# A two-layer decoder kernel: router jobs in three units, shorter fillers, and a third set of split expert weights made two passes ahead

## The reference

```python
x = ln(x + self_attention(x))                 # 4 heads
x = ln(x + cross_attention(x, ctx))           # 16 heads
x = ln(x + moe_0(x))                          # 8 experts, top 2, F = 1024
x = ln(x + state_space(x))                    # h = exp(d*A)*h + (d*x)*B ; y = h.C
x = ln(x + linear_attention(x, ctx))          # softmax over keys, k^T v, q (k^T v)
# last sub-layer: 8 experts, top 2, F = 512, and one expert that all tokens pass
probs = softmax(xt @ Wg); topv, topi = top_k(probs, 2); topv /= topv.sum()
y  = gelu(xt @ Wu[e]) @ Wd[e]                 # for the two chosen e
x  = ln(x + gelu(xt @ W1) @ W2 + sum(topv * y))
```

## Time and profile before

| | us |
|---|---|
| median of 3 runs (lowest, highest) | 1577.16 (1569.95, 1578.38) |
| the profiled execution | 1579.87, its span 1578.1 |
| state-space units, from the first scan to the last | 1025 to 1287 |
| tail of the state-space stage | 1287 to 1318 |
| `m1`, first transpose on PE to the end | 1318 to 1578 |
| `m1`, routed double tiles (transposes of tile 10 to those of tile 24) | 1391 to 1516 |

### The profile page before, as it was taken

One profiled execution on the slowest core, in us unless ns is written; L12 is line 12 of the kernel. 1 busy time (PEld: TensorE's weight loads), 2 busy tenths in 40 slices (PEclk: granted clock), 3 DMA queues, 4 the chain that ended last, 5 costly groups with the idle time before them and its releaser, 6 DMA issues.

```text
span 1578.1 us, 27783 instructions
## 1 busy us (share of the span) xinstructions
PE 1387.3 (88%) x9328; PEld 1122.2 (71%) x9328; DVE 1100.6 (70%) x2430; ACT 933.1 (59%) x2302; POOL 828.2 (52%) x866
## 2 busy tenths in 40 slices
PE   4788999999999999966999999778989989998891
PEld 3566677777777777654999999445556558988881
DVE  4677866666666766647688884599989964766535
ACT  4666565655655655532688871277778843466553
POOL 3665454444444444531688872278868761265540
PEclk9889999999999999956999999989999999999896
DMA  4100000000000000045566568645443411245574
GB/s 147 41 28 7 21 15 8 2 7 2 8 8 1 8 1 2 1 142 221 184 235 218 206 220 295 243 147 162 142 128 129 140 46 54 94 161 180 182 246 174
DMA packets 52943, 167.87 MB, mean 106 GB/s; under 512 B 13178, under 2 KB 22340, under 8 KB 44996
## 3 DMA queue, kind: packets, MB, share of 16 engines
q1 hardware_dynamic: 45316, 145.63, 26.4%
q0 software_dynamic: 7488, 20.46, 4.0%
HBM read 149.28 MB, written 16.78 MB: 105 GB/s over the span
## 4 chain that ended last, share of the span: by engine, by line
PE 34%; DVE 7%; POOL 6%; issue 5%; ACT 4%; DMA 1%; POOLq 0%; DVEq 0%; SPq 0%; ACTq 0%
PE m_ps L1751 10%; PE m_ps L1774 10%; POOL s_hc L2073 4%; PE m_ps L1748 2%; PE m_ps L1769 2%; PE s_yps L2504 1%; PE m_ps L1731 1%; DVE s_h L2439 1%; PE s_dps L2615 1%; ACT s_dps L2152 1%; PE s_yps L2610 1%; DVE tokens L1619 1%; PE s_jps L2538 1%; PE m_ps L1699 1%; PE m_ps L1655 0%
## 5 line engine op out<-in xcount | busy, mean ns | idle before, releaser
L306 POOL TENSOR_TENSOR a_pexp<-a_pexp,a_rsum 128x384 f32<-128x384 f32 (+1 forms) x320 | 246.4, 788 | 303.3 <-DVE a_rsum L523 303.3
L396 ACT ACTIVATE a_pexp<-a_ps,a_nmax 128x384 f32<-128x384 f32 (+1 forms) x320 | 181.1, 566 | 171.8 <-DVE a_nmax L519 171.2
L519 DVE TENSOR_REDUCE a_nmax<-a_ps 128x1 f32<-128x384 f32 (+1 forms) x320 | 153.9, 522 | 71.8 <-PE a_ps L620 70.8
L2073 POOL TENSOR_TENSOR s_hc<-s_h,s_bc_rows 128x1024 f32<-128x1024 f32 x64 | 151.2, 2366 | 55.6 <-DVE s_h L2439 53.0
L1751 PE MATMUL m_ps<-m_xT,m_w1s 128*128 128x256 f32 x960 | 151.2, 297 | 16.6 <-issue 13.3
L2439 DVE TENSOR_TENSOR_SCAN s_h<-s_dps,s_inp 128x512 f32<-128x512 f32 x128 | 148.8, 1204 | 0.0
L1751 PEld LDWEIGHTS m_ps<-m_xT,m_w1s 128*128 128x128 f32 x960 | 133.9, 203 | 19.3 <-issue 15.1
L636 PE MATMUL a_ps<-a_ident,a_pexp 128*128 128x128 f32 x896 | 144.7, 274 | 3.4 <-ACT a_pT L255 3.0
L1099 POOL DMA_INDIRECT m_xrow<-table,m_row_from x78 | 81.1, 1040 | 125.7 <-DVE m_row_from L1446 90.1
L1774 PE MATMUL m_ps<-m_w2s,m_hs 128*128 128x256 f32 x960 | 143.1, 285 | 0.0
L2504 PE MATMUL s_yps<-s_hc,s_ident 128*128 128x512 f32 x256 | 124.5, 609 | 12.4 <-POOL s_hc L2073 12.0
(11 more groups left out here) (450 smaller groups left out, 3660.0 us busy)
## 6 DMA issues: line engine op xcount, KB each, us to landing
s_bc_rows<-s_bc_table SPq DMA_DIRECT2D x64, 512.0 KB, 3.7
arrived<-in_down SPq DMA_DIRECT2D x29, 1024.0 KB, 6.4
arrived<-in_up SPq DMA_DIRECT2D x23, 1024.0 KB
m_w<-in_up SPq DMA_DIRECT2D x16, 512.0 KB
m_w<-in_down SPq DMA_DIRECT2D x16, 512.0 KB
carried_up<-in_up SPq DMA_DIRECT2D x8, 512.0 KB, 5.5
carried_down<-in_down SPq DMA_DIRECT2D x8, 512.0 KB, 6.2
arrived<-results SPq DMA_DIRECT2D x3, 1024.0 KB, 8.5
```

Source lines behind the costliest of these rows:

```text
L306: nc.gpsimd.tensor_tensor(pexp[:, r, 0:n], pexp[:, r, 0:n], rsum[:, r:r + 1].to_broadcast([128, n]), ALU.mult).then_inc(normed, 1)
L396: nc.scalar.activation(pexp[:, r, 0:n], ps_s[score_bank(u)][:, 0:n], ACT.Exp, bias=nmax[:, r:r + 1], accum_out=sums[:, r:r + 1]).then_inc( ...
L519: nc.vector.tensor_reduce(nmax[:, u % RING:u % RING + 1], ps_s[score_bank(u)][:, 0:keys_of(u)], AX.X, ALU.max, negate=True).then_inc(maxed, 1)
L2073: nc.gpsimd.tensor_tensor(halves(hc[:, u % HC_RING, :]), halves(h[:, u % H_RING, :]), bc_rows[:, u % BC_RING, 1, :].unsqueeze(1).to_broadc ...
```

## The change

Three edits. The router's jobs G0, G1 and H stand in three units, G0 of chunk c - 1 in unit 15, G1 of chunk c - 2 in unit 0, H of chunk c - 2 in unit 4; for chunk 2, G0 is in unit 63 and G1 and H both in the tail. The fillers of the tail are 2 and 9 dummy matmuls, not 10 and 20. In the second expert layer there are three sets of split weights, and chunk ft of tile j + 2 is cast and subtracted in pass j, not that of tile j + 1. The first expert layer keeps two sets and one pass.

```diff
+    W_SETS = 3 if shared else 2
+    LOOK = W_SETS - 1
...
-        w1s = [... for b in range(2)]
+        w1s = [... for b in range(W_SETS)]
...
-            return (n, n // 2, n % 2) if routed(j) else (0, 0, 0)
+            return (n, n // 2, n % W_SETS) if routed(j) else (0, 0, 0)
...
             if shared:
-                for c in range(FT):
-                    low_part(TILES_SHARED, c)
+                for n in range(LOOK):
+                    for c in range(FT):
+                        low_part(TILES_SHARED + n, c)
...
-                    if j + 1 < TILES:
-                        low_part(j + 1, c)
+                    if j + LOOK < TILES:
+                        low_part(j + LOOK, c)
...
-                        act_e.wait_ge(h_used, tile * FT + 1)
+                        act_e.wait_ge(h_used, (tile + 2 - W_SETS) * FT + 1)
...
-                    if new_weights(j + 1):
-                        high_part(weights_of(j + 1), j + 1, ft)
+                    if new_weights(j + LOOK):
+                        high_part(weights_of(j + LOOK), j + LOOK, ft)
...
-                    if new_weights(j + 1) and on_dve(weights_of(j + 1)[0], ft) and split_weights(weights_of(j + 1)[0]):
+                    if new_weights(j + LOOK) and on_dve(weights_of(j + LOOK)[0], ft) and split_weights(weights_of(j + LOOK)[0]):
...
-        LOGITS_AT, COLUMNS_AT = 0, 15
+        ROUTER_JOBS = {15: ("G0", 1), 0: ("G1", 2), 4: ("H", 2)}
...
+        def router_jobs_at(u):
+            return [(job, u // N - behind) for job, behind in [ROUTER_JOBS[u % N]] if u // N >= behind] if u % N in ROUTER_JOBS else []
...
-                if c >= 2 and n == LOGITS_AT:
-                    logits(c - 2)
...
-                if c >= 1 and n == COLUMNS_AT:
-                    for half in range(2):
-                        router_columns(c - 1, half)
+                for job, of in router_jobs_at(u):
+                    router(job, of)
...
             for job in BEHIND_JOBS.values():
                 behind(CH - 1, job)
                 if job == "Y1":
-                    logits(LAST - 1)
-                    occupy(10)
-            occupy(20)
+                    router("G1", LAST - 1)
+                    router("H", LAST - 1)
+                    occupy(2)
+            occupy(9)
```

More of the change, by code:

```diff
@@ L865, in moe_layer @@
             w2 = [weight_bufs[:, (W_BUFS + b) * KD * F:(W_BUFS + b + 1) * KD * F].rearrange("p (f d) -> p f d", f=FT) for b in range(W_BUFS)]
-        w1s = [carried["up_parts"] if shared and b == 0 else [sb(f"w1s{b}{h}", [128, KD, F], fp32r)[:] for h in range(2)] for b in range(2)]
-        w2s = [carried["down_parts"] if shared and b == 0 else [sb(f"w2s{b}{h}", [128, FT, D], fp32r)[:] for h in range(2)] for b in range(2)]
+        w1s = [carried["up_parts"] if shared and b == 0 else [sb(f"w1s{b}{h}", [128, KD, F], fp32r)[:] for h in range(2)] for b in range(W_SETS)]
+        w2s = [carried["down_parts"] if shared and b == 0 else [sb(f"w2s{b}{h}", [128, FT, D], fp32r)[:] for h in range(2)] for b in range(W_SETS)]
         b1 = sb("b1", [128, B_BUFS, FT])
@@ L1912, in jobs_at @@
         def jobs_at(c, n):
[L1914 removed]
+            return ([f"{AHEAD_JOBS[n]}.{c + 1}"] if n in AHEAD_JOBS and c + 1 < CH else []) + ([f"{BEHIND_JOBS[n]}.{c - 1}"] if n in BEHIND_JOBS and c >= 1 else [])
         SEQS, ND = T // S, S // 128
@@ L1929, in state_space_and_linear_layers @@
         for u in range(UNITS):
-            JOBS += jobs_at(u // N, u % N) + [f"{job}.{b}" for job, b in linear_jobs_at(u)] + ([f"G{half}.{u // N - 1}" for half in range(2)] if u % N == COLUMNS_AT and u >= N else [])
-        JOBS += [f"Y0.{LAST}", f"Y1.{LAST}", f"H.{LAST - 1}"] + [f"{j}.{LAST}" for j in BEHIND_JOBS.values() if j[0] != "Y"]
+            JOBS += jobs_at(u // N, u % N) + [f"{job}.{b}" for job, b in linear_jobs_at(u)] + [f"{job}.{c}" for job, c in router_jobs_at(u)]
+        JOBS += [f"Y0.{LAST}", f"Y1.{LAST}", f"G1.{LAST - 1}", f"H.{LAST - 1}"] + [f"{j}.{LAST}" for j in BEHIND_JOBS.values() if j[0] != "Y"]
         NUMBER = {j: i for i, j in enumerate(JOBS)}
@@ L2223, in logits, with router @@
                 nc.scalar.copy(carried["logits"][:, c * TC:(c + 1) * TC, :], b[:, 0:TC * E].rearrange("p (t e) -> p t e", t=TC)).then_inc(j_act, 1)
+            def router(job, c):
+                if job == "H":
+                    logits(c)
+                else:
+                    router_columns(c, int(job[1]))
             def high_part(n):
```

4 lines of the change are left out of this document (2 added, 2 removed).

## The result

The kernel after takes **1561.03 us** in the median (1552.87 to 1565.32), the kernel before 1578.38 on the same chip (1569.95 to 1586.6): a ratio of 0.9889, with a 95% interval of 0.9868 to 0.991. It is 1.1% faster, 17.5 us of 1577, with 14 to 21 in the interval. The forecast was -21.5, 1556. One execution of this study, of the kernel of experiment 10, ran in a slow state (2245.61 us at a mean granted clock of 0.554); the ratios leave it out, and the median there is 1552.43 with it and 1550.62 without. The profiled execution after has a span of 1557.8, before 1578.1, so 20.3 less.

What follows compares the result with a forecast made beforehand. PE was taken as the bound, losing time to late split weights, half clock and tail dummies. Terms -13 (third set), -1.5 (router jobs) and -7 (tail) gave -21.5 from the median 1577.16, say 1556 us; range 1542 to 1571.

Steps and rivals of the forecast that it cites:

- Third set, -13: Routed double tiles: PE's waits for split weights shrink, 9.8 us, and the clock returns 3.3; bounds 3 to 25.
- In its place more ahead of L1774: Sign in the 15 passes: more idle time ahead of down matmuls, released by DVE, replacing waits for up weights.
- POOL's low part blocks its gathers behind it as before: Double tiles: gathers still queue behind POOL's low part, only in the other parity; costed at nothing.
- Loads and passes 6 and 7, at nothing: Second expert layer: earlier loads keep their two-pass lead and the casts fit in passes 6 and 7; no cost.
- Router jobs, -1.5: State-space units: splitting the jobs over three units removes PE's 1.27 us wait; gain 2.5 at most, loss 1.5 at most.
- Tail, -7: Between the stages: fewer dummies bring -3 us up to the end of Z and -4 at the second filler.
- (a): Double tiles: late completions move stalls to down matmuls, gain only 3, total 1566; chance 0.24 with the third set's failure.
- (b): Double tiles: all waits and clock loss go, 6.6 us a pass, -25, total 1544; chance 0.09.
- (c): Tail: X, Z and second filler at half clock, tail gains nothing, first passes lose 4, total 1567; chance 0.06.
- (d): Double tiles: gathers served after the weight load bring rows late, +16 us, total 1593; chance 0.04.

Runs made afterwards that it cites:

- experiment 10: Kernel after with rows split before weights, gathers before POOL's low part, no POOL low parts from the second tile, and no fillers: 1552.43 us, ratio 0.9837.
- experiment 1: Kernel before with the third set of split weights alone, router jobs and fillers as before: 1570.64 us, ratio 0.9955.
- experiment 4: Kernel after with three sets of split weights, but each made only one pass ahead: 1566.54 us, ratio 0.9933.
- experiment 6: Kernel after with chunk 3 made by DVE, so no low parts on POOL from the second tile on: 1545.57 us, ratio 0.9809.
- edit 7: Kernel after with each gather issued half a pass earlier, ahead of POOL's low part, in both expert layers: 1550.68 us, ratio 0.9844.
- experiment 5: Kernel after with the split of the rows ahead of the weights' chunk on ACT and DVE, both expert layers: 1558.33 us, ratio 0.9884.
- experiment 9: Kernel after with rows split before weights, gathers before POOL's low part, and no POOL low parts from the second tile: 1554.74 us, ratio 0.9854.
- experiment 12: Kernel after without POOL's two products of the digits with the slot weights (results get other weights): 1558.7 us, ratio 0.9892.

## Why the prediction was right, and where it was not

**Third set, -13: right in kind, too large in size.** The profiled passes gained 12.0, the runs 7.1 (experiment 1; 6.9 as the difference of the kernel after and experiment 4). As to the size, the trace after shows passes at the short end of their kind (112.7 of 112.7 to 115.5), so its 12.0, so near to the forecast, is in part luck. The waits for `m_w1s` went, 14.5 to 2.3 (forecast: below 3). The clock gave back 3.2 (forecast 3.3), and the stretches at the lower level begun in the passes are three for five. That a lead is what counts, not a buffer, is shown by experiment 4. Two lines of the step did not hold. "In its place more ahead of L1774" did not come in the trace after, 4.0 as before, though it did with the third set alone, 7.8. And "POOL's low part blocks its gathers behind it as before", costed at nothing, is where the gain ended: rows were late in four places, 4.8 us. Experiments 6 and 7 take that wait to nothing and are worth 13 and 7 us. That is more than the idle time: in experiment 6 PE's busy time in the passes fell by 6.4 us with the clock at its upper level throughout.

**Loads and passes 6 and 7, at nothing.** No load was late: ACT's casts, which wait for them, stood idle for 0.0 us. From tile 8 to tile 10, passes 6 to 8, the stretch grew by 3.5. Two edits of the three, alone, and a third set without lead have it as well, and the third set alone has not; so it belongs to no part of the change. It depends on when DVE's subtraction meets POOL's products. In the kernel before, a subtraction began at 1379.42, just before the first product ended at 1379.67, and passed between the two in 0.80 us; the second product then took 2.67 instead of 2.34, and PE waited 0.67. No row that the prediction used shows that POOL and DVE can block each other, though that trace holds one at 1381.11, 1.86 us long, and 26 more in the first expert layer.

**Router jobs, -1.5: -2.4** in the trace, -2.2 (from +0.6 to -5.0) in the runs; inside the bounds. The gap of 1.27 ahead of G is gone.

**Tail, -7: -6.9.** Y to X gained 4.2 (forecast 3.4 to 5.8), Z at the lower clock took back 1.7 of the 3.4 set aside, the second filler gave 4.4 (forecast 4). `m1` starts 0.3 us after the last normalised rows. Alone the fillers are worth 8.8 (5 to 12): no smaller than forecast. Over all traces the stretch from the last scan to tile 0 took 30.2 to 33.5 us with the old fillers and 23.7 to 26.6 with the new, so both profiled executions stand at the long end and their difference is a fair one. What the step left was the first filler: experiment 10 puts 2.2 us on it.

**Rivals.** (a), that completions take the place of the weights, fell with the 12.0, but experiment 5 shows it in part (13.0 us ahead of down matmuls). (b), all of it, was not this change, but experiment 9 has it: 99.64 us is the 6.6 a pass that it named. What was held against it was POOL's time; the engine was the right one, but its order counted as much: edit 7 keeps all its work and still has 104.8. (c), the clock, cost 1.7 and not the whole tail. (d), late rows, was held to be 4 in 100 and a matter of all or nothing; it came in small.

**The sum.** 1561 instead of 1556: the third set was taken 6 too large by the runs, the fillers 2 and the jobs 1 too small.

## What to carry to other kernels

Work made earlier pays by its lead, not by its buffer; once the wait is gone, look at what shares the queue of the engine that helped, here gathers behind a low part on POOL. Put what the next stage waits for first on each engine, and keep VectorE's two-SBUF-operand work and GpSimd's elementwise work apart in time: here one collision cost 3 us of PE, and an order with more of them went with 4 to 12 us in the first expert layer. Put dummy matmuls only into a gap that the data leaves, and no longer than it. An edit in code that two stages share is two edits; read both stages.

## What the runs showed of the hardware

In the second expert layer a subtraction of two SBUF tiles on DVE took 1.5 to 2.9 us instead of 0.68 when a product or a low part of POOL, both of which read SBUF, held it. In both expert layers of all 14 traces, every such subtraction over 0.8 us, 347 in number, ended 0.54 to 0.56 us after a POOL instruction ended; with a PSUM operand it took 0.69 beside the same POOL instruction. The order of the starts in the records is no proof of who holds the ports: in experiment 12 DVE's record starts 0.13 us before POOL's, and DVE waited. ACT starts on a finished matmul group up to 6.3 us late in the 15 passes (1444.97 in the kernel after), by over 0.8 us not once in passes 0 to 6, without transfers from POOL, and with 0.28 instead of 0.70 of DMA share as often (13 times). Without fillers, 4.07 us of idle PE were followed by 10.2 us at the lower clock; with the second filler in that place the clock there stayed at its upper level (experiment 9).
